# First cross-attention of a Perceiver kernel: each chunk of keys in two units, each of one narrow burst and one wide run

## The reference, cut to what matters

```python
def _L0_xattn_ref(input_q, input_k, wq, wk, wv):   # 16 heads, D_K = 64, 16 values a head
    q = (input_q @ wq).reshape(B, LQ, N_HEADS, D_K).transpose(0, 2, 1, 3)
    k = (input_k @ wk).reshape(B, LK, N_HEADS, D_K).transpose(0, 2, 1, 3)
    v = (input_k @ wv).reshape(B, LK, N_HEADS, D_V_HEAD).transpose(0, 2, 1, 3)
    attn = jnp.einsum('bhqd,bhkd->bhqk', q, k) / jnp.sqrt(jnp.float32(D_K))
    attn = jax.nn.softmax(attn, axis=-1)
    out = jnp.einsum('bhqk,bhkd->bhqd', attn, v)
```

## Time and profile before

| | us |
|---|---|
| median of 3 runs (lowest, highest) | 972.09 (971.97, 972.6) |
| span of the profiled execution, first to last instruction | 969.2 |
| PE busy | 945.4 |
| DVE busy | 692.3 |
| ACT busy | 587.2 |
| POOL busy | 373.8 |

### The profile page before, as it was taken

The page is one execution under the profiler, slowest core; times in us unless marked ns, Lnnn a source line. Parts: engine busy times, 40 slices in busy tenths (PEclk is TensorE's granted clock), DMA queues, the critical chain, the costliest instruction groups (busy, mean ns, idle before and its releaser), DMA issues.

```text
span 969.2 us, 30871 instructions
## 1 busy us (share of the span) xinstructions
PE 945.4 (98%) x13321; PEld 696.8 (72%) x13321; DVE 692.3 (71%) x876; ACT 587.2 (61%) x1404; POOL 373.8 (39%) x406
## 2 busy tenths in 40 slices
PE   6999999999999999999999999988999999999998
PEld 5666666666666666666666666667987787889998
DVE  3788878888878888888877877785026554467886
ACT  5677766666667666666666766632236663336664
POOL 2344444444444444444434344330113331513332
PEclk9999999999999999999999999999999999999999
DMA  6100001010000011001000000029848988508992
GB/s 234 27 24 23 24 25 24 24 25 24 24 25 24 24 24 25 24 24 25 24 16 12 24 24 3 4 86 400 283 156 262 278 276 299 174 1 297 323 336 94
DMA packets 78552, 98.08 MB, mean 101 GB/s; under 512 B 21584, under 2 KB 56928, under 8 KB 78432
## 3 DMA queue, kind: packets, MB, share of 16 engines
q1 hardware_dynamic: 77344, 94.67, 30.3%
q10 hardware_dynamic: 1088, 1.57, 0.5%
HBM read 95.68 MB, written 0.13 MB: 99 GB/s over the span
## 4 chain that ended last, share of the span: by engine, by line
PE 81%; DVE 8%; ACT 5%; issue 4%; POOL 2%; DMA 0%; ACTq 0%; DVEq 0%; POOLq 0%
PE ps L360 29%; PE ps L383 18%; PE ps L393 9%; PE ps L367 7%; PE ps L1521 6%; PE ps L997 3%; PE ps L1538 2%; PE ps L1542 2%; PE ps L1539 2%; ACT x_pr L1163 2%; DVE c1T_lo L1201 2%; DVE x_negc L1207 1%; ACT c1T_hi L1157 1%; DVE x_negm L1210 1%; ACT x_prT L1171 1%
## 5 line engine op out<-in xcount | busy, mean ns | idle before, releaser
L553 ACT ACTIVATE probs<-ps,x_peak 128x512 f32<-128x512 f32 (+1 forms) x400 | 269.6, 678 | 177.7 <-DVE x_peak L618 167.0
L618 DVE TENSOR_REDUCE x_peak<-ps 128x2 f32<-128x1024 f32 (+1 forms) x200 | 237.1, 1186 | 93.3 <-PE ps L383 93.3
L637 DVE STREAM_TRANSPOSE probsT<-probs 128x1024 f32<-128x1024 f32 (+1 forms) x200 | 242.9, 1215 | 12.6 <-ACT probs L553 12.1
L383 PE MATMUL ps<-keys,qT 64*32 64x512 f32 (+1 forms) x3200 | 195.2, 584 | 2.2 <-ACTq L559 1.6
L360 PE MATMUL ps<-ctxT_hi,wk_hi 128*128 128x512 f32 (+1 forms) x400 | 162.8, 407 | 0.8 <-ACT keys L543 0.8
L799 POOL TENSOR_SCALAR vals<-vals_t,x_side 128x512 f32<-128x512 f32 (+1 forms) x100 | 152.4, 1542 | 6.9 <-PEq L407 4.2
L360 PE MATMUL ps<-ctxT_lo,wk_hi 128*128 128x512 f32 (+1 forms) x400 | 154.8, 387 | 0.0
L360 PE MATMUL ps<-ctxT_hi,wk_lo 128*128 128x512 f32 (+1 forms) x400 | 153.9, 385 | 0.0
L360 PEld LDWEIGHTS ps<-ctxT_hi,wk_hi 128*128 128x128 f32 x400 | 75.1, 188 | 73.6 <-issue 39.8
L543 ACT COPY keys<-ps 128x512 f32<-128x512 f32 (+1 forms) x200 | 110.4, 577 | 27.5 <-PE ps L360 19.6
L765 POOL TENSOR_TENSOR ctxT_lo<-ctx_raw,ctxT_hi 128x512 fp32r<-128x512 f32 x48 | 61.7, 1287 | 133.8 <-ACT ctxT_hi L539 133.8
(11 more groups left out here) (256 smaller groups left out, 1302.9 us busy)
## 6 DMA issues: line engine op xcount, KB each, us to landing
m_w<-in_m_w SPq DMA_DIRECT2D x32, 1024.0 KB, 7.8
ctx_raw<-in_ctxT SPq DMA_DIRECT2D x24, 512.0 KB, 3.7
ctx_two<-in_ctxT SPq DMA_DIRECT2D x24, 512.0 KB, 4.0
ctx_one<-in_ctx SPq DMA_DIRECT2D x24, 512.0 KB, 5.1
x_shrinkT<-x_shrink SPq DMA_DIRECT2D x384, 1.0 KB, 1.7
f_h1T<-in_f_h1T SPq DMA_DIRECT2D x1, 4096.0 KB, 18.1
f_h2T<-in_f_h2T SPq DMA_DIRECT2D x1, 4096.0 KB, 27.9
m_shared_w<-in_m_sw SPq DMA_DIRECT2D x2, 1024.0 KB, 7.9
```

What stands on the lines that cost most here:

```text
L383: i = pe.matmul(m.ps[32 * j:32 * (j + 1), 2 * (t % 2) + odd, 0:nt * P], m.qT[rows, 4 * group + j, qs], m.keys[slot][rows, 4 * group + j, 0 ...
L553: i = act.activation(m.probs[t % 2][:, odd, 0:nt * P], m.ps[:, 2 * (t % 2) + odd, 0:nt * P], ACT.Exp, bias=m.peak[slot][:, 1, 2 * (t // 4) ...
L618: dv.tensor_reduce(m.peak[slot][:, 1, cs, t % 4], m.ps[:, 2 * (t % 2):2 * (t % 2) + 2, 0:nt * P], AX.X, ALU.min).then_inc(s["dve" if t == ...
L637: i = dv.transpose(m.probsT[slot][:, cs, 0:4 * nt, t % 4 * 32:t % 4 * 32 + 32], m.probs[t % 2][:, :, 0:nt * P].rearrange("p c (b k) -> p c ...
```

## The change: what it does

A chunk becomes two units. PE's unit is one narrow burst: three score steps, half the weighting of the chunk before, the fourth score step. Then one wide run of five groups: in the first unit four key groups of this chunk (pairs 4 to 7) and its second value group, in the second unit four key groups of the next chunk (pairs 0 to 3) and its first value group. Score steps now use banks 0/1, 2/3, 6/7 and 0/1 again (`SCORE_BANKS`), the wide groups and the weighting share banks 4 and 5 (`WIDE_BANK`), so the weighting of each unit is transposed and added on its own, before the wide run. The keys have one buffer in place of two, the probabilities three in place of two. DVE takes three maxima in a row, then the sum, then one transposition, the fourth maximum and the other three transpositions. ACT takes three steps of exponentials, a key copy, the fourth step with a key copy between its halves, a cast of the context, two key copies. POOL splits its setting aside and its context parts over the two units, and adds twice a chunk. The tail chunk has a hand-written order of its own on each engine (not shown: PE does keys 0 to 3, scores 0 and 1, keys 4 and 5, scores 2 and 3, keys 6 and 7, both value groups, scores 4 and 5, keys 0 and 1 of the next chunk, scores 6 and 7, keys 2 and 3 and the first value group). The last chunk is two units without wide work at the end, followed by the old last weighting.

```diff
-    m.keys = [m.new(f"keys{i}", [PAIRS, CHUNK]) for i in range(2)]
+    m.keys = m.new("keys", [PAIRS, CHUNK])
+    below_queries = m.at + 16 * KIB
+    m.probs = [m.new("probs2", [2, CHUNK])]
+    m.at = below_queries
     m.qT = m.new("qT", [PAIRS, P])
...
-    m.probs = [m.new(f"probs{i}", [2, CHUNK]) for i in range(2)]
+    m.probs = [m.new(f"probs{i}", [2, CHUNK]) for i in range(2)] + m.probs
...
-VALUES, KEYS_AHEAD = {0: (0, 1)}, {2: (0, 1, 2), 4: (3, 4), 6: (5, 6, 7)}
-WEIGHT_STEPS, FIRST_KEYS = (0, 4), 6
-TURN_STEPS, SPLIT_STEPS, SUM_STEP = (2, 2), (5, 7), 7
-KEEP_BETWEEN, KEEP_AFTER = {0: 5, 4: 0}, {1: (6, 7), 5: (1, 2), 6: (3,), 7: (4,)}
-
-
...
+HALF = STEPS // 2
+SCORE_BANKS, PROB_SLOTS = (0, 2, 6, 0), (0, 1, 2, 0)
+WIDE_BANK, LAST_BANK = 4, 4
...
+    def wide(slot, first_pair, half, nt):
+
+        for q in range(HALF):
+            if q >= 2:
+                pe.wait_ge(s["k_kept"], n("k_kept"))
+            key_group(slot, first_pair + q, nt)
+        value_group(slot, half, nt)
 
...
-    def scores(slot, t, nt):
-        group, qs = t // 4, slice(t % 4 * 32, t % 4 * 32 + 32)
+    def scores(t, nt):
+        group, qs = t // HALF, slice(t % HALF * 32, t % HALF * 32 + 32)
         for j in range(4):
             for odd, rows in enumerate((TOP, LOW)):
-                i = pe.matmul(m.ps[32 * j:32 * (j + 1), 2 * (t % 2) + odd, 0:nt * P], m.qT[rows, 4 * group + j, qs],
-                              m.keys[slot][rows, 4 * group + j, 0:nt * P], start=True, stop=True,
-                              skip_group_check=True)
+                i = pe.matmul(m.ps[32 * j:32 * (j + 1), SCORE_BANKS[t % HALF] + odd, 0:nt * P],
+                              m.qT[rows, 4 * group + j, qs], m.keys[rows, 4 * group + j, 0:nt * P],
+                              start=True, stop=True, skip_group_check=True)
         i.then_inc(s["scores_full"], 1)
 
...
+    def context_free(ahead):
+        pe.wait_ge(s["ctx_split"], n("ctx_split", 2))
+        if ahead > 1:
+            pe.sem_inc(s["raw_free"], 1)
+
+    def unit(slot, half, nt, nt_before, ahead):
+
+        pe.wait_ge(s["k_kept"], n("k_kept"))
+        pe.wait_ge(s["scores_read"], n("scores_read", 3))
+        for t in range(3):
+            scores(HALF * half + t, nt)
+        values_turned()
+        if half == 0:
+            pe.wait_ge(s["probs_turned"], n("probs_turned"))
+            pe.wait_ge(s["vals_ready"], n("vals_ready"))
+        weighted(1 - slot, range(2 * nt_before * half, 2 * nt_before * (half + 1)))
+        pe.wait_ge(s["scores_read"], n("scores_read"))
+        scores(HALF * half + 3, nt)
+        pe.wait_ge(s["out_kept"], n("out_kept"))
+        pe.sem_inc(s["out_turned"], 1)
+        if half == 0:
+            wide(slot, HALF, 1, nt)
+        elif ahead:
+            context_free(ahead)
+            wide(1 - slot, 0, 0, CHUNK_TILES)
+
+    def chunk(slot, nt_before, ahead):
+        for half in range(2):
+            unit(slot, half, CHUNK_TILES, nt_before, ahead)
+
...
-    def chunk(slot, nt, nt_before, ahead):
-        for t in range(0, STEPS, 2):
-            if t == FIRST_KEYS:
-                pe.wait_ge(s["k_kept"], n("k_kept"))
-            for u in (t, t + 1):
-                pe.wait_ge(s["scores_read"], n("scores_read"))
-                scores(*step_after(slot, u, nt, ahead, 2))
-            for half in VALUES.get(t, ()):
-                values(slot, half, nt)
-            for p in KEYS_AHEAD.get(t, ()):
-                next_keys(slot, p, ahead)
-            if nt_before:
-                if t == 0:
-                    pe.wait_ge(s["probs_turned"], n("probs_turned"))
-                    pe.wait_ge(s["vals_ready"], n("vals_ready"))
-                if t in WEIGHT_STEPS:
-                    first = 2 * nt_before * WEIGHT_STEPS.index(t)
-                    weighted(1 - slot, range(first, first + 2 * nt_before), 4 * nt_before - 1)
-                if t == STEPS - 2:
-                    pe.wait_ge(s["out_kept"], n("out_kept"))
-                    pe.sem_inc(s["out_turned"], 1)
...
+        pe.wait_ge(s["probs_turned"], n("probs_turned"))
+        pe.wait_ge(s["vals_ready"], n("vals_ready"))
+        weighted(slot, range(4 * nt), (0, 1), "last_full")
         pe.wait_ge(s["acc_whole"], 1)
+        pe.wait_ge(s["scores_read"], n("scores_read", 2))
...
+    def unit(slot, half, split, first_pair, signal="alpha_ready"):
+
+        for t in range(HALF * half, HALF * half + 3):
+            exponentials(slot, t, CHUNK_TILES)
+        if first_pair is not None:
+            keep_keys(first_pair, CHUNK_TILES)
+        exponentials(slot, HALF * half + 3, CHUNK_TILES, None if first_pair is None else first_pair + 1)
+        if half == 1:
+            shrink_factors(slot, signal)
+        if split is not None:
+            split_context(split, 1 - half, CHUNK_TILES)
+        if first_pair is not None:
+            for p in (first_pair + 2, first_pair + 3):
+                keep_keys(p, CHUNK_TILES)
+
+    def chunk(slot):
+        unit(slot, 0, 1 - slot, HALF)
+        unit(slot, 1, slot, 0)
+
...
+    def unit(slot, half, order, signals=(STEPS - 1,)):
+
+        first = HALF * half
+        turn_values(slot, half, CHUNK_TILES)
+        if half == 0 and order >= 2:
+            dv.wait_ge(s["rescaled"], n("rescaled"))
+        for t in range(first, first + 3):
+            maxima(slot, t, CHUNK_TILES)
+        if half == 1 or order >= 2:
+            dv.wait_ge(s["acc_added"], n("acc_added"))
+        turn_out()
+        turn_probabilities(slot, first, CHUNK_TILES)
+        maxima(slot, first + 3, CHUNK_TILES)
+        for t in range(first + 1, first + HALF):
+            turn_probabilities(slot, t, CHUNK_TILES, signals)
+
+    def chunk(slot, order, signals=(STEPS - 1,)):
+        for half in range(2):
+            unit(slot, half, order, signals)
+
...
+    def unit(slot, half, split, signal="acc_added"):
+
+        set_aside(slot, half, CHUNK_TILES)
+        if half == 0:
+            rescale(1 - slot)
+        add_out(1 - slot, signal)
+        if split is not None:
+            split_context(split, 1 - half)
+
+    def chunk(slot):
+        unit(slot, 0, 1 - slot)
+        unit(slot, 1, slot)
+
```

More of the change, by code:

```diff
@@ L392, in weighted @@
                 for two, rows in enumerate((TOP, LOW)):
-                    i = pe.matmul(m.ps[32 * c:32 * (c + 1), 6 + two, 0:P], m.vals[slot][rows, b, c, :],
-                                  m.probsT[slot][rows, c, b, :], start=(b == 0), stop=(b == last),
+                    i = pe.matmul(m.ps[32 * c:32 * (c + 1), WIDE_BANK + two, 0:P], m.vals[slot][rows, b, c, :],
+                                  m.probsT[slot][rows, c, b, :], start=(b == blocks[0]), stop=(b == blocks[-1]),
                                   skip_group_check=True)
-            if b == last and signal:
-                i.then_inc(s[signal], 1)
-    def values(slot, half, nt):
-        pe.wait_ge(s["k_kept"], n("k_kept"))
-        for i in range(TERMS):
-            done = value_term(slot, half, nt, i)
-        done.then_inc(s["v_full"], 1)
+        i.then_inc(s[signal], 1)
     def values_turned():
@@ L558, in exponentials @@
-        i.then_inc(s["probs_ready"], 1)
-        act.drain().then_inc(s["scores_read"], 1)
-    def chunk(slot, nt, ahead, first=False):
-        for t in range(2 if first else 0, STEPS):
-            keys = 1 - slot if t > 1 else slot
-            kept = t < 2 or ahead
-            exponentials(slot, t, nt, (keys, KEEP_BETWEEN[t]) if kept and t in KEEP_BETWEEN else None)
-            if t == STEPS - 1:
-                act.wait_ge(s["below_ready"], n("below_ready"))
-                act.activation(m.shrink[slot][:, :, :, :], m.below[:, :, :, :],
-                               ACT.Exp).then_inc(s["alpha_ready" if ahead else "alpha_last"], 1)
-            if kept:
-                for p in KEEP_AFTER.get(t, ()):
-                    keep_keys(keys, p, CHUNK_TILES)
-            if ahead > 1 and t in SPLIT_STEPS:
-                split_context(slot, SPLIT_STEPS.index(t), CHUNK_TILES)
@@ L588, in xattn0_scalar @@
-    exponentials(0, 0, TAIL_TILES)
-    keep_queries(1)
-    for p in range(4, 6):
-        keep_keys(0, p, TAIL_TILES)
-    exponentials(0, 1, TAIL_TILES)
-    for p in range(6, 8):
-        keep_keys(0, p, TAIL_TILES)
-    for k in range(DK):
-        split_context(1, k, CHUNK_TILES)
-    chunk(0, TAIL_TILES, 2, first=True)
-    chunk(1, CHUNK_TILES, 2)
+        exponential(slot, t, 0, nt)
+        if between is not None:
+            keep_keys(between, CHUNK_TILES)
+        exponential(slot, t, 1, nt).then_inc(s["probs_ready"], 1)
```

394 lines of the change are left out of this document (203 added, 191 removed).

## The result

The kernel after the change takes 975.69 us (median of 5 runs, 973.69 to 976.96), the kernel before 972.42 beside it; the ratio is 1.0034, 95% interval 1.0022 to 1.0045. I had predicted 963.0 (953 to 975) and faster; it is slower by 0.3%.

What follows compares the result with a forecast made beforehand. PE, busy 98%, was taken as the limit. 33.8 + 25.0 + 22 x 25.26 + 12.5 + 11.6 = 638.6 to the last weighting, against 647.58 before: 9.0 us off, so 963.0 us, range 953 to 975.

Steps and rivals of the forecast that it cites:

- the part on PE: PE in each chunk: same products in two bursts of 5.40 and two wide runs of 7.03, 24.86 us before waits.
- the 0.04 by which the mean chunk before exceeds its pattern: Old kernel's chunks: mean 25.64 against a pattern of 25.60 us; the 0.04 was added to each new chunk.
- Switching, 0.74 a chunk: PE between narrow and wide work: fewer changes per chunk, so 24.86 us before waits, 0.74 less than before.
- The rival that it isn't saved: PE's narrow work pays the switching instead: chunk 25.60 plus 0.36, 17 us more, 980; chance 0.05.
- Value group late by 0.11 and 0.25: Wide run's value group waits for ACT's third key copy: 0.11 us in first units, 0.25 in second, 0.36 a chunk.
- The dearer value for the weight load: After PE's wait before the value group, the weight load cannot go ahead: 0.10 us more; without it chunks are 25.02.
- The rival without lateness: Value group never waits, since ACT needs 0.2 us less: chunks of 24.90, total 954.9; chance 0.23.
- A burst over 5.6 as a sign of being wrong: PE's narrow bursts were to be 5.4 us long, two a chunk; over 5.6 would refute the forecast.
- Chunk of 25.26: Each of 22 full chunks on PE: 24.86 plus 0.36 of waits plus 0.04, in us.
- Evacuation as the bound: Chain from first maximum to third key copy on DVE and ACT delays PE 0.37 us a unit, 980.4; chance 0.25.
- POOL's cover: POOL's rescaled sum is added by about 12.8, DVE asks at 17.2: 4.4 us of cover, no wait.
- Ends: First full chunk's start at 33.8, within 1 us; PE's last weighting 11.6 us after the last burst starts; rest unchanged.

Runs made afterwards that it cites:

- e2: Changed kernel with 8 spare products (32 PE instructions) at the front of the program; 967.67 us, ratio 0.9964.
- e7: Changed kernel with ACT's third key copy ahead of factors and context cast, plus 4 spare products (16 instructions) in front; 959.71 us, ratio 0.9877.
- e9: Changed kernel, ACT's order untouched, with 12 spare products (48 PE instructions) in front; 965.17 us, ratio 0.9937.
- e6: Changed kernel with ACT's third key copy ahead of factors and context cast, plus 12 spare products (48 instructions) in front; 954.89 us, ratio 0.9821.
- e3: Changed kernel with ACT's third key copy moved ahead of factors and context cast, nothing in front; 966.46 us, ratio 0.995.
- e12: Changed kernel without shift, each full unit weighting only six of its eight key blocks (64 PE instructions fewer); 964.46 us, ratio 0.9915.
- e4: Kernel before the change with 8 spare products (32 PE instructions) in front, as control; 974.0 us, ratio 1.0026.
- e10: Kernel before the change with 12 spare products (48 PE instructions) in front, as control; 975.42 us, ratio 1.0034.
- e11: Changed kernel with ACT's third key copy first, plus 28 products of 32 columns (112 instructions) in front; 968.33 us, ratio 0.9958.

## Why the prediction was wrong

**The step that failed** is the first of the part on PE: "Products, columns and types stay the same", with a burst built from the rows of its parts as 5.40. I counted what PE computes and not how fast its instructions arrive. Every row that I added up was true; what the sum left out is that the change puts all the narrow work of a half chunk, 384 instructions, in one burst of 5.4 us, where before at most 320 stood together. Per instruction, products of 128 columns in 64x32 tiles are the shortest of a chunk: 256 instructions in 1.75 us (starts at 333.35 and 335.10), against 29 us (128 x 0.227) of wide products. The kernel before had shown the effect once, as a block of 8.81 in place of 7.98, which I took for part of the mean ("the 0.04 by which the mean chunk before exceeds its pattern", 0.88 over 22 chunks, and this block alone is 0.83 of it) and did not ask about.

**How a stop arises,** as the stops of the kernel after, e2 and e7 have it. The packet starts at 334.21, 328.43 and 324.98, and the loads go on 2.2, 2.4 and 2.6 later, at load 16 of the fourth step, load 128 of the weighting, and load 8 of the fourth step. The border one block (128 loads) earlier then lies at load 16 of the weighting, load 16 of the third score step and load 8 of the weighting. PE's loads pass it at 333.4, 327.9 and 324.8, so the packet starts 0.8, 0.5 and 0.2 behind that. Over the 11 stops of the kernel after between 60 and 600 it starts 0.15 to 0.81 behind, and the loads go on 2.6 to 3.3 behind the border.

How long would PE take for these 128 loads without a stop? The loads of e9, which has none, tell:

```profile
275.67 0.15 PEld L387 LDWEIGHTS ps<-keys,qT 64*32 64x32 f32 x8 [0.28 <-issue]
276.96 1.73 PEld L397 LDWEIGHTS ps<-probsT,vals 64*32 64x32 f32 x120 [0.28 <-issue]
278.59 0.32 PEld L387 LDWEIGHTS ps<-keys,qT 64*32 64x32 f32 x16
```

From border to border it is 1.8 us at the place of the kernel after, 2.15 at that of e7, 2.4 at that of e2, and 2.8 at its own, from load 8 of the third score step (275.72) to load 120 of the weighting (278.51). In this order the waits shrink: 0.7 to 1.45 in the kernel after, about 0.6 or less in e7, 0.87 or less in e2 and mostly under 0.5, none in e9. In e9 the packet starts at 275.63, so the next border is reached 2.9 behind it: just late enough.

What counts is the time from the packet's start, and not only that from border to border. The kernel before passes a whole block in 1.77 us (loads at 247.95 and 249.72) and doesn't stop. Its border lies just behind a wide run, and the packet came at 245.77, while PE's loads were still in that run:

```profile
245.77 0.19 PEld L367 LDWEIGHTS ps<-ctxT_lo,wv_hi 128*128 128x128 f32 x1
247.91 1.76 PEld L393 LDWEIGHTS ps<-probsT,vals 64*32 64x32 f32 x128 [0.35 <-issue]
```

A packet can start up to 44 instructions before the loads reach the border (the most in any of these traces). That is 5 us of a wide run (22 x 0.227), but 0.3 of the weighting (22 x 0.0137). So the kernel before stood at a good place: the packets for its fastest blocks started while PE was still at wide products.

Two counts over all traces bear this out. I numbered PE's instructions in the order of its program, loads, products and semaphore instructions as they are recorded. From 60 to 620, inside a burst, loads wait 54 times for issue by 0.5 us or more, in nine of the fourteen traces, in both orders of the work, and each time it is number 193 or 194 of 256, counted from 0 at the program's start. (The first load of a burst is left out; it has waits of its own.) And nowhere in the fourteen traces does the load behind a border start sooner than 2.17 us after the start of its packet. That a packet brings what stands behind the *next* border is inferred from these times; what PE's queue holds, the trace doesn't show.

The Trainium skill, "Runtime: NRT & Kernel Launch", section "Instruction fetch mechanics", has the mechanism: blocks of 16 KiB with 256 instructions, fetched over a DMA queue of the sequencer's own while the current ones run. The trace agrees, 105 packets of 16 KB for 26,942 instructions. The section also says that the cost is mostly hidden, since instructions are dispatched more slowly than they are fetched. Here the measurement decides otherwise: in a burst they are used faster. By the page alone, e9's time would be the time of every shift.

**Point by point.**
- *Switching, 0.74 a chunk.* Right. With no wait a unit was to take 12.43; e6 has 12.44 and 12.50, and burst and wide run of the kernel after are 5.44 and 7.18 where 5.40 and 7.03 plus the wait were predicted. The rival that it isn't saved (chance 0.05) is excluded.
- *Value group late by 0.11 and 0.25.* Right, 0.13 and 0.27 by e3, and for the reason named. The dearer value for the weight load holds too: behind ACT's copy the second product starts 0.34 after the first (329.16 to 329.50), in e3 0.23 (299.00 to 299.23), so in the first unit nearly all of the loss is this 0.11 and not the wait. The rival without lateness (0.23) falls in this kernel and is what e3 makes.
- *A burst over 5.6 as a sign of being wrong.* It came: in a long unit the wide run starts 6.64 behind the burst (330.75 to 337.39), in 11 of 45 units.
- *Chunk of 25.26.* 25.34 in e9, 25.84 in the kernel after. From first to last full burst it took 606.45 us (34.56 to 641.01), in e9 594.68: 11.8 more.
- *Evacuation as the bound* (0.25). Not in this kernel: from 60 to 600 PE waits for neither DVE nor ACT where a wide run starts or a fourth score step does; only the value group waits for ACT, as forecast. But e12 shows how near it is: of the 0.43 that its burst is shorter, about three quarters don't come off the unit (0.07 and 0.15 do), and the waits named there are most of that.
- *POOL's cover* of 4.4 held: no wait of PE on POOL from 60 to 600.
- *Ends.* First full burst at 34.56 for 33.8, within the 1 us given; the last weighting 11.5 behind the last burst (641.01 to 652.53) for 11.6, and then 322.7 to the end of the span, 1.1 more than before.

Added up, the last weighting starts at 652.53 rather than 638.6: 11.6 from the long units, 1.6 from short units of 25.34 rather than 25.26 a pair, 0.8 from the start. The range missed it because no case in it made PE itself slower on the same products. The sign came out wrong, too, by the place alone: the kernel before stood at a good place for its order, the kernel after at a bad one. With the same instructions in front of both, run side by side, the changed kernel is faster: 967.67 against 974.0 with 32 (e2, e4), 965.17 against 975.42 with 48 (e9, e10). The last is about 1%, where 0.9% was forecast. Which place each kernel came to stand at was chance: nothing in the prediction spoke for one or the other, and at e9's place the forecast would have looked right without its author knowing of the stops.

Left open: why a packet starts sometimes 0.2 and sometimes 0.8 us behind the same border, and with it why long units of one trace differ by 0.7 (13.53 to 14.24).

## What to carry to other kernels

Where TensorE runs hundreds of very small products together, count instructions as well as columns: divide 256 by their rate, and if it comes under 3 us (here the loads behind a border came 2.2 to 3.0 us after the start of their packet where PE stood for them), look for weight loads that stand for "issue" for a microsecond with a packet of the instruction queue ahead. Such a stop depends on the place in the program, so two versions are compared fairly only if each is tried with some 16, 32 and 48 instructions in front; a difference of 0.3% at one place, of either sign, says nothing about the order of the work. And a block that is longer than its neighbours once in a trace is worth a look before its excess is averaged in.

## What the runs showed of the hardware that I had not expected

- 48 instructions without use in front of the program took 10.5 us off the changed kernel (975.69 to 965.17) and put about 3 on the kernel before (ratio 1.0034).
- 16 semaphore increments between matmuls keep PE for 0.9 us, 0.06 each, against 0.007 for a product or a load of the weighting (1.75 over 256).
- A float32 product with 128x128 weights takes 0.22 us a record at the start of the program whether it has 32 columns or 128: padding with narrow products is no cheaper there. This holds for the slower stretch at the start only; from 8.16 on a record of 128 columns takes 0.13 in e6 (2.05 over 16).
- A packet can also start much later than 0.2 to 0.8 us behind its border. In e12 the border 128 loads before the last stop is load 30 of the last weighting, passed at 635.05; the packet starts at 638.20, and PE goes on 5.6 us behind the border. In e11 it is 639.95, 642.79 and 5.1. The DMA engines were taking in weights both times (in e12 a share of 0.58 from 635 and 1.01 from 637.5, rows above; in e11 0.48 from 639 to 642.5), so queueing behind them suggests itself. It isn't shown: e12 has packets 2.0 to 2.9 us behind their border in the attention as well, with a share of 0.09 from 60 to 600. There the border lies in a score step (passed at 289.21, packet at 291.47).
